# A decoder layer's cross-attention: the second batch's value sums as one group of 14 tiles, and one block of self scores ahead of the value products

## The reference: three small cross-attentions and a decoder of six layers

```python
def _mha(s, t, kv_w, q_w, o_w, o_b, mask):
    k, v = jnp.split(s @ kv_w, 2, axis=-1)
    q = t @ q_w
    k, v, q = (_heads(k), _heads(v), _heads(q))
    scores = jnp.einsum('bhqd,bhkd->bhqk', q, k) * D ** (-0.5)
    scores = jnp.where(mask[:, None] == 0, jnp.float32(-1000000000.0), scores)
    attn = jax.nn.softmax(scores, axis=-1)
    o = jnp.einsum('bhqk,bhkd->bhqd', attn, v)
    return o.transpose(0, 2, 1, 3).reshape(t.shape[0], t.shape[1], H * D) @ o_w + o_b

def step(t, p):
    tn = _ln(t, norm_g, norm_b)
    t = _mha(tn, tn, skv, sq, sow, sob, tgt_mask) + t     # self-attention, 112 keys
    tn = _ln(t, norm_g, norm_b)
    t = _mha(src, tn, ckv, cq, cow, cob, src_mask) + t    # cross-attention, 375 keys of 128 features
    tn = _ln(t, pg, pb)
    t = t + (jax.nn.relu(tn @ w1 + b1) @ w2 + b2)
    return (t, None)
```

## Time and profile before

| what | value |
|---|---|
| median of 3 runs | 3053.2 us (3051.46 to 3053.27) |
| the profiled execution | 3047.71 us, of which its span 3045.8 us |
| TensorE products busy | 2852.7 us (94%) |
| TensorE weight loads busy | 2316.1 us (76%) |
| VectorE busy | 1679.2 us (55%) |
| ScalarE busy | 1303.0 us (43%) |
| GpSimd busy | 963.0 us (32%) |
| granted clock of TensorE, mean | 0.984 of full speed |

### The profile page before, as it was taken

How to read it: one execution, slowest core, us unless ns; L and a number is a source line. 1 busy time by engine, 2 the same in 40 slices (tenths; PEclk the granted TensorE clock), 3 DMA queues, 4 the chain that set the end, 5 groups by cost and what they waited for, 6 DMA issues and landing times.

```text
span 3045.8 us, 69468 instructions
## 1 busy us (share of the span) xinstructions
PE 2852.7 (94%) x23656; PEld 2316.1 (76%) x23656; DVE 1679.2 (55%) x6361; ACT 1303.0 (43%) x4274; POOL 963.0 (32%) x1169
## 2 busy tenths in 40 slices
PE   6675899999999999999999999999999999999999
PEld 4454678878878878778778778778778778878877
DVE  2343546546546546546546546646656655655655
ACT  2122335435435435435445445445444444444444
POOL 0000333323323323324324324323323323333333
PEclk9797899999999999999999999999999999999999
DMA  5102010030211031211021211022111022111010
GB/s 157 27 0 83 1 28 14 15 86 19 81 28 22 8 86 26 74 28 28 2 86 36 64 28 28 2 86 55 45 28 28 2 86 68 32 28 28 1 28 14
DMA packets 132257, 120.64 MB, mean 40 GB/s; under 512 B 15261, under 2 KB 121318, under 8 KB 130278
## 3 DMA queue, kind: packets, MB, share of 16 engines
q1 hardware_dynamic: 131942, 116.53, 14.9%
HBM read 115.59 MB, written 0.92 MB: 38 GB/s over the span
## 4 chain that ended last, share of the span: by engine, by line
issue 49%; POOL 25%; PE 21%; DVE 2%; ACT 1%; POOLq 1%; DMA 0%; SPq 0%; DVEq 0%; ACTq 0%
POOL prob L541 18%; PE proj L581 8%; PE proj L601 3%; POOL prob L511 3%; PE sum L601 3%; PE sum L769 2%; POOL ctx_parts L532 1%; PE proj L573 1%; POOL tw L491 1%; PE score L745 1%; PE tr L756 1%; DVE qcT L1191 1%; PE score L581 1%; POOLq L540 1%; POOL ctx_parts L529 1%
## 5 line engine op out<-in xcount | busy, mean ns | idle before, releaser
L541 POOL TENSOR_TENSOR prob<-prob,rtotal 128x375 f32<-128x375 f32 x672 | 543.5, 812 | 746.9 <-DVE rtotal L1451 745.9
L961 ACT ACTIVATE prob<-prob,negmax 128x375 f32<-128x375 f32 (+1 forms) x688 | 418.8, 609 | 453.6 <-DVE negmax L1442 423.3
L884 PE MATMUL sum<-pT,ctx 32*128 32x224 f32 (+1 forms) x4608 | 500.7, 358 | 12.6 <-DVE qcT L1434 12.6
L884 PE MATMUL tr<-pT,ctx 32*128 32x224 f32 (+1 forms) x4608 | 500.7, 359 | 0.0
L884 PEld LDWEIGHTS sum<-pT,ctx 32*128 32x128 f32 (+1 forms) x4608 | 417.8, 185 | 73.0 <-issue 73.0
L1442 DVE CUSTOM_DVE_ANT_0 prob<-score,cbias 128x375 f32<-128x375 f32 x672 | 357.7, 532 | 195.3 <-PE score L581 193.7
L884 PEld LDWEIGHTS tr<-pT,ctx 32*128 32x128 f32 (+1 forms) x4608 | 417.2, 185 | 0.0
L581 PE MATMUL score<-ctx_parts,qc_high 128*128 128x376 f32 x1344 | 412.3, 388 | 0.0
L1460 DVE STREAM_TRANSPOSE pT<-prob 128x384 f32<-128x384 f32 x672 | 373.2, 558 | 0.0
L511 POOL TENSOR_TENSOR prob<-prob,rtotal 112x448 f32<-112x448 f32 x200 | 186.4, 932 | 574.2 <-DVE rtotal L1318 574.2
L1032 ACT ACTIVATE prob<-prob,negmax 112x112 f32<-112x112 f32 x800 | 298.9, 377 | 86.3 <-DVE negmax L1336 86.3
(11 more groups left out here) (170 smaller groups left out, 4785.2 us busy)
## 6 DMA issues: line engine op xcount, KB each, us to landing
ctx<-ctx SPq DMA_DIRECT2D x192, 176.0 KB
w_kv<-sa_kv SPq DMA_DIRECT2D x6, 2048.0 KB, 10.0
f<-ff_w SPq DMA_DIRECT2D x12, 1024.0 KB, 7.6
cmask<-ctx_mask SPq DMA_DIRECT2D x24, 375.0 KB, 4.2
w_q<-sa_q SPq DMA_DIRECT2D x6, 1024.0 KB, 11.2
w_o<-sa_ow SPq DMA_DIRECT2D x6, 1024.0 KB, 5.7
c_q<-ca_q SPq DMA_DIRECT2D x6, 1024.0 KB, 8.2
c_o<-ca_ow SPq DMA_DIRECT2D x6, 1024.0 KB, 10.7
```

The source lines that it names most:

```text
L541: pool.tensor_tensor(row, row, rtotal[:, G * SG + i:G * SG + i + 1].broadcast_to([P, S2]), ALU.mult).then_inc(prob_ready, 1)
L884: ins = pe.matmul(bank[:, 0:HT * R], ctx4[keys_of, m // (HALVES // NB), j, :], pT[keys_of, m % 2, :, j * R:(j + 1) * R], start=j == 0, sto ...
L961: act.activation(o, i, ACT.Exp, bias=negmax[0:rows, col:col + 1], scale=scale, accum_out=total[0:rows, col:col + 1]).then_inc(exp_ready, 1)
```

## The change

The four groups of 7 tiles become three: two of 7 for batch 0, at the steps they had, and one of 14 for batch 1 after the loop (steps 31, 32, 33 in a row, products of 14 x 32 = 448 columns, one wait for all 28 transposes). The seventh query chunk moves from step 28 to 25 and the eighth from 30 to 28. `self_scores(at, 1)` moves from behind the value products to in front of them, behind the last sums. The value products wait once, for the copies of the whole third group; ACT and DVE each make two copies of 448 columns there in place of four of 224. `pT` holds 14 tiles as before, without the division in halves, and tile i of the second batch takes the place of tile i of the first.

```diff
-    HALVES = 4
-    HT = NT // HALVES
+    PARTS = ((0, 0, TB // 2), (0, TB // 2, TB // 2), (1, 0, TB))
+    LAST = [TB // 2, TB, NT]
...
-    QUERY_STEPS = {t: c for c, t in enumerate((14, 16, 17, 19, 21, 23, NT, NT + 2))}
-    SUM_STEPS = {HT * m + t: (m, i) for m in range(HALVES - 1) for i, t in enumerate((11, 13, 15))}
-    SUM_STEPS.update({NT + 4 + i: (HALVES - 1, i) for i in range(PIECES)})
-    TAKE_STEPS = {HT * m + 16: m for m in range(HALVES - 2)}
+    QUERY_STEPS = {t: c for c, t in enumerate((14, 16, 17, 19, 21, 23, 25, NT))}
+    SUM_STEPS = {t: (m, i) for m, steps in enumerate(((11, 13, 15), (18, 20, 22), (NT + 3, NT + 4, NT + 5)))
+                 for i, t in enumerate(steps)}
+    TAKE_STEPS = {16: 0, 23: 1}
     SCORE_0 = NT + 1
...
-                                pe.wait_ge(turned, at.at("turned", HT * (m + 1)))
+                                pe.wait_ge(turned, at.at("turned", LAST[m]))
...
-                                    ins = pe.matmul(bank[:, 0:HT * R], ctx4[keys_of, m // (HALVES // NB), j, :],
-                                                    pT[keys_of, m % 2, :, j * R:(j + 1) * R],
+                                    b, first, n = PARTS[m]
+                                    ins = pe.matmul(bank[:, 0:n * R], ctx4[keys_of, b, j, :],
+                                                    pT[keys_of, first:first + n, j * R:(j + 1) * R],
                                                     start=j == 0, stop=j == KB - 1)
...
+                    self_scores(at, 1)
                     weights("c_v")
                     for c in range(HC):
-                        if c % (HC // 2) == 0:
-
-                            m = HALVES // NB + c // (HC // 2)
+                        if c == 0:
+
                             for name in SUM_BANKS:
-                                pe.wait_ge(taken[name], at.emptied(name, BEFORE_SUMS[name] + m + 1))
+                                pe.wait_ge(taken[name], at.emptied(name, BEFORE_SUMS[name] + len(PARTS)))
...
-                    self_scores(at, 1)
                     weights("c_o")
...
-                    contexts(2)
+                    queries(at, HC - 1)
                     self_maxima(at, 0)
                     self_maxima(at, 1)
-                    queries(at, HC - 1)
                     self_reciprocals(at, 0)
-                    contexts(3)
+                    contexts(2)
```

More of the change, by code:

```diff
@@ L100, in attention_layers @@
     PIECES = 3
-    assert ROWS % P == 0 and TB % (HALVES // NB) == 0 and KB % PIECES == 0 and HT * P == ROWS // 2
+    assert ROWS % P == 0 and NB == 2 and TB * R <= 512 and KB % PIECES == 0
     DUOS = SG // 2
     KEY_STEPS = {t: c for c, t in enumerate((1, 2, 3, 4, 6, 7, 9, 10))}
-    QUERY_STEPS = {t: c for c, t in enumerate((14, 16, 17, 19, 21, 23, NT, NT + 2))}
-    SUM_STEPS = {HT * m + t: (m, i) for m in range(HALVES - 1) for i, t in enumerate((11, 13, 15))}
-    SUM_STEPS.update({NT + 4 + i: (HALVES - 1, i) for i in range(PIECES)})
-    TAKE_STEPS = {HT * m + 16: m for m in range(HALVES - 2)}
+    QUERY_STEPS = {t: c for c, t in enumerate((14, 16, 17, 19, 21, 23, 25, NT))}
+    SUM_STEPS = {t: (m, i) for m, steps in enumerate(((11, 13, 15), (18, 20, 22), (NT + 3, NT + 4, NT + 5)))
+                 for i, t in enumerate(steps)}
+    TAKE_STEPS = {16: 0, 23: 1}
     SCORE_0 = NT + 1
-    END = NT + 4 + PIECES
+    END = NT + 3 + PIECES
     SUM_Q = 2
@@ L115, in attention_layers @@
     MAIN = {"proj0": V2 + QC_FILLS + HC + CV_FILLS + 1 + FC // 2 + 1, "proj1": FF_OUT + 1, "score0": (SG + NT) // 2,
-            "score1": (SG + NT) // 2, "tr0": QC_FILLS + HALVES + SG // 2, "tr1": QC_FILLS + HALVES + SG // 2,
-            "sum0": 1 + HALF + HALVES + DUOS // 2, "sum1": 1 + HALF + HALVES + 1 + DUOS // 2 + 1,
+            "score1": (SG + NT) // 2, "tr0": QC_FILLS + len(PARTS) + SG // 2, "tr1": QC_FILLS + len(PARTS) + SG // 2,
+            "sum0": 1 + HALF + len(PARTS) + DUOS // 2, "sum1": 1 + HALF + len(PARTS) + 1 + DUOS // 2 + 1,
             "stats": 3, "tn": 3 * NB, "resid": 3, "negmax": SG + NT, "exp": SG + NT,
@@ L131, in __init__ @@
             self.self_0 = NT if part == 2 else 0
-            self.tr_0 = QC_FILLS + HALVES if part == 2 else 0
+            self.tr_0 = QC_FILLS + len(PARTS) if part == 2 else 0
         def base(self, name):
@@ L223, in attention_layers @@
         prob = sb("prob", [P, PROBS, G * S])
-        pT = sb("pT", [P, 2, HT, S2B])
-        probT = pT[0:KR, 0, :, :].rearrange("p t k -> p (t k)")[:, 0:2 * KJ * G * S]\
+        pT = sb("pT", [P, TB, S2B])
+        probT = pT[0:KR, :, :].rearrange("p t k -> p (t k)")[:, 0:2 * KJ * G * S]\
             .rearrange("p (n j s) -> p n j s", n=2, j=KJ)
@@ L239, in context_rows @@
         def context_rows(m, g):
-            b, first = m // (HALVES // NB), m % (HALVES // NB) * HT * P
-            return cT[:, b, first:first + HT * P].rearrange("p (t q) -> p t q", q=P)[:, :, g * R:(g + 1) * R]
+            b, first, n = PARTS[m]
+            return cT[:, b, first * P:(first + n) * P].rearrange("p (t q) -> p t q", q=P)[:, :, g * R:(g + 1) * R]
         FW = 2 * EK * E + 2 * E
@@ L890, in _ @@
                             for i in range(2):
-                                pe.wait_ge(taken[f"proj{i}"], at.emptied(f"proj{i}", at.n[f"proj{i}"] - 1 + i))
+                                pe.wait_ge(taken[f"proj{i}"], at.emptied(f"proj{i}", at.n[f"proj{i}"] - i))
                             self_scores(at, 0)
+                    self_scores(at, 1)
                     weights("c_v")
                     for c in range(HC):
-                        if c % (HC // 2) == 0:
-                            m = HALVES // NB + c // (HC // 2)
+                        if c == 0:
                             for name in SUM_BANKS:
-                                pe.wait_ge(taken[name], at.emptied(name, BEFORE_SUMS[name] + m + 1))
+                                pe.wait_ge(taken[name], at.emptied(name, BEFORE_SUMS[name] + len(PARTS)))
                         name = f"proj{c // 2 % 2}"
@@ L1109, in contexts @@
                             bank = filled(at, name)
-                            copy(context_rows(m, g), bank[:, 0:HT * R].rearrange("p (t q) -> p t q", q=R)).then_inc(taken[name], 1)
+                            copy(context_rows(m, g), bank[:, 0:PARTS[m][2] * R].rearrange("p (t q) -> p t q", q=R)).then_inc(taken[name], 1)
                     for t in range(NT):
@@ L1120, in _ @@
                             contexts(TAKE_STEPS[t])
-                    queries(at, HC - 2)
+                    self_exponentials(at, 0)
                     contexts(2)
-                    self_exponentials(at, 0)
-                    contexts(3)
                     chunk(at, oT[:, 0:2, :].rearrange("p c t -> p (c t)"), 2 * T2)
@@ L1433, in contexts @@
                             bank = filled(at, name)
-                            dve.tensor_copy(context_rows(m, g), bank[:, 0:HT * R].rearrange("p (t q) -> p t q", q=R))\
+                            dve.tensor_copy(context_rows(m, g), bank[:, 0:PARTS[m][2] * R].rearrange("p (t q) -> p t q", q=R))\
                                 .then_inc(taken[name], 1)
@@ L1453, in _ @@
                             i = t - TURN_LAG
-                            m = i // HT
-                            if i % HT == 0 and m >= 2:
+                            if i >= TB and i - TB in (0, TB // 2):
                                 for name in SUM_BANKS:
-                                    gate(ready[name], at.at(name, BEFORE_SUMS[name] + m - 1))
+                                    gate(ready[name], at.at(name, BEFORE_SUMS[name] + (i - TB) // (TB // 2) + 1))
                             dve.wait_ge(prob_ready, at.at("prob", i + 1))
-                            dve.transpose(pT[:, m % 2, i % HT, :], prob[:, i % PROBS, 0:S2B]).then_inc(turned, 1)
+                            dve.transpose(pT[:, i % TB, :], prob[:, i % PROBS, 0:S2B]).then_inc(turned, 1)
                         if KEY_STEPS.get(t, 0) % 2 == 1:
```

1 line of the change is left out of this document (removed).

## The result

| | median (range), runs | profiled execution | span | granted clock |
|---|---|---|---|---|
| before | 3053.23 us (3051.46 to 3058.52), 4 | 3047.71 | 3045.8 | 0.984 |
| changed | 3097.81 us (3094.27 to 3100.83), 4 | 3100.83 | 3099.0 | 0.978 |

The ratio is 1.0143 with a 95% interval of 1.0125 to 1.016. The forecast was 3092, in a range of 3069 to 3110.

What follows compares the result with a forecast made beforehand. TensorE, busy 94% of the span, was taken as the bound. Saved switching against new idle time made each pair 1.64 us longer; 24 x 1.64 = 39 on 3053.2 gave 3092 us, range 3069 to 3110.

Steps and rivals of the forecast that it cites:

- The sums (9.28): The merged third group's 24 passes of 448 columns on TensorE: 9.28 us, bounds 9.18 and 10.0.
- Steps 2 to 4: TensorE waits for DVE's maxima before tile 26's scores (0.35 us), tile 27's (0.48) and the first self scores (0.6).
- Step 5: Before the merged sums TensorE waits for all 28 transposes: 1.5 us idle, starting at 1525.47.
- Step 7: Value products wait for the third group's wide copies: 1.44 us, 0.97 hidden by self scores, 0.47 idle.
- The sum: Over tile 25's scores to the output projection, each pair gets 1.64 us longer; 24 pairs make 39 us.
- check by kinds: Per pair: saved 0.9 us switching and 0.6 before a piece; new idle time 3.4; the rest called rounding.
- the clock rival: Sparse work before the sums lowers TensorE's clock: 2.6 us a pair, 3155 us, or 3102 in one of six; chance 0.10.
- clock 1.00 throughout: Sign that the forecast is right: granted clock stays at 1.00.
- a clock of 0.5 inside a pair: Sign that the forecast is wrong: the granted clock falls to 0.5 within a pair.
- The switches decide: Only TensorE's work counts in the stretch, with fewer split-array sections: 1.73 us less a pair, 3012 us; chance 0.05.
- Later waits take it up: The 1.43 us wait before L573 absorbs the delay: 0.2 a pair, 3058 us, no change; chance 0.03.
- The tail is shorter: DVE's pace and the copies hide half of the delay: 0.8 us a pair, 3072 us; chance 0.12.

Runs made afterwards that it cites:

- experiment 1: The changed kernel with the second self scores moved back behind the value products: 3123.98 us, ratio 1.0238 to the kernel before.
- Experiment 2: The changed kernel with two useless products between the first self scores and the wait for the last transposes: 3087.15 us, ratio 1.0121 to the kernel before.
- experiment 3: The changed kernel with the eighth query chunk moved from behind tile 27's scores to behind tile 26's: 3127.74 us, ratio 1.0245 to the kernel before.
- experiment 5: The kernel before with group 2's three pieces directly behind tile 27's scores, group 3 apart, seventh query chunk at step 25: 3036.6 us, ratio 0.9958.
- experiment 6: The kernel before with group 2 gathered behind tile 27's scores, seventh query chunk at step 25, eighth behind tile 26's scores: 3021.27 us, ratio 0.99.

## Why the prediction was right, and where it was not

**What bounds.** Right for the 1.54 a pair: TensorE is busy 0.65 less in the stretch and idle 2.19 more. The slow pairs' loss is not idle time but busy time at the lower clock, and the page's equal busy times (2852.7 and 2853.8) hide both.

**The sums (9.28).** 1671.98 to 1681.21 is 9.23, and wide passes start 0.38 apart, for 0.19. A product twice as wide costs twice as much here. The estimate of 0.187 counts two clock periods a column without saying so (224 columns at 2.4 GHz are 0.093 with one); only the lower bound of 9.18 hangs on it, for the sum goes by the measured 0.189.

**Steps 2 to 4.** On the prediction's axis tile 26's scores start at 1519.91 (forecast 1519.95), tile 27's at 1520.91 (1520.95), the first self scores at 1523.00 (1523.0).

**Step 5.** The sums start at 1525.34 for 1525.47: from tile 27's maximum to the last transpose 2.96 pass, as before, but TensorE follows in 0.05, not 0.14. That the chain runs through exponential, reciprocal and POOL's product was argued from the order of the rows; no run shortened one of its links, so which of them sets the 2.96 stays open.

**Step 7.** The bare wait is 0.50, forecast 0.47, and experiment 1 shows the rest of it under the self scores. From the end of the sums to the value products 1.54 pass, forecast 1.44: DVE's last copy ends at 1682.50, and TensorE starts 0.25 behind it, not 0.14. The Trainium skill's page on tiling ("TensorEngine Tiling (Array Packing)", Performance Considerations, PSUM Bottleneck) warns that the copies out of PSUM may become the limit after such packing; the trace agrees, for the four wide banks that fill at one moment leave TensorE 1.47 a pair without work in experiment 1.

**The sum.** 1.54 a pair for 1.64, 37 for 39 us. Experiment 2, in which nothing else is late, measures it alone: 36.8. The check by kinds gives 3.4 - 0.9 - 0.6 = 1.9, and the 0.26 to 1.64 is not rounding, as the prediction has it: 0.20 of it is the seventh chunk, which the walk takes at 0.75 where the kernel before pays 0.95.

**The step that failed** is the weight of the clock rival: "The clock falls", given 0.10, with one pair in six as its mild form. The forecast's sum has nothing for it, and "clock 1.00 throughout" stands among its signs; a clock of 0.5 inside a pair, one of the prediction's own signs of being wrong, is what came. It came beside the forecast and not in its place: 8 pairs of 24 in the profiled execution, 1.69 each where I had 2.6. I had called 51% of work from 1519.60 to 1525.47 an argument against it, although the emptiest part, 0.97 us of work in some 3, lies inside. Rows at either level and experiments 2 and 3 decide. The Trainium skill bears on it: by "TensorE: Matmul & The Clock Gate", Part 1, the gate goes by how busy the engine has been of late, and the runs agree, with 0, 8 and 15 slow pairs as that place gets emptier. Luck has a part in how near 3092 came to 3098: the waits were 0.1 a pair too long (2 us too many), and the clock, some 8 us in the medians, was missing. How many slow pairs the other executions had isn't recorded; (44.6 - 37) / 1.69 would be about five, an estimate.

**The other rivals.** *The switches decide* fell: the waits are there. Its saving is real, though. In experiments 5 and 6, where cover is kept, a pair's stretch is 0.53 and, with the chunk moved, 1.21 shorter; of this 0.37 and 0.83 are less busy time (54.30 a pair before, 53.93 and 53.47 there) and the rest less idle time. *Later waits take it up* fell: the wait at L573 is 34.3 in 24 before and after. *The tail is shorter* fell as well.

## What to carry to other kernels

Work that looks as if it only interrupts a chain may be what hides it. Before several pieces are gathered at the end, ask which inputs each piece needs: the group that needs only old ones goes first, behind the last scores, and covers the softmax for the one that needs the last. When two copies or sums are merged into one, the first half's cover is lost too; price that wait. And look at the emptiest stretch that a change leaves on TensorE, not at its mean, for the clock may fall there and the next dense stretch pays.

## What the runs showed of the hardware that I had not expected

- Filling 0.95 us of an idle stretch in every pair (1.30 to 0.35) with useless products made the kernel faster: 37 against 45 us above its kernel before, slow pairs 0 in place of 8.
- The fall of the clock is not the same in every pair, though all have the same order and the same idle time in the pair's stretch to 0.04 us: the slow pairs of the changed kernel are the 2nd, 3rd, 5th to 7th and 9th to 11th of 24, and none after. In experiment 1 they are the 2nd, 7th, 11th, 13th, 15th, 19th and 24th. What picks them stays open.
- Between DVE's last transpose and TensorE's first sum only 0.05 us pass; behind a copy out of PSUM of 224 columns it was 0.14, behind one of 448 columns 0.25.
